# A graph network's attention node stage in five steps a chunk, with the table's bias as a product of a row of ones

## The reference, cut to what matters

```
h = jnp.maximum(_layernorm(x, axis=-1), 0.0)
x = x + _L1_gnn_ref(h, edge_index, ...)      # attention over edges and over each node's own loop, then elu
h = jnp.maximum(_layernorm(x, axis=-1), 0.0)
x = x + _L2_gnn_ref(h, edge_index, W, b)     # its first step is h @ W + b, a table with a row for each node
```

## Time and profile before

| | |
|---|---|
| Median of three runs | 5364.16 us (5360.74 to 5365.61) |
| The profiled execution, its own time | 5366.58 us |
| Its span in the trace | 5364.8 us, clock 0.893 of full speed in the mean |
| The phase of the change, first DMA issue to the next phase's first | 2806.41 to 2995.83 us, 189.4 us or 3.5% of the span |
| 13 chunks in it, from one `attention` to the next | 12.45 us in the mean |

### The profile page before, as it was taken

The page is one execution under the profiler, slowest core; times in us unless marked ns, Lnnn a source line. Parts: engine busy times, 40 slices in busy tenths (PEclk is TensorE's granted clock), DMA queues, the critical chain, the costliest instruction groups (busy, mean ns, idle before and its releaser), DMA issues. The chain is left out here.

```text
span 5364.8 us, 105914 instructions
## 1 busy us (share of the span) xinstructions
PE 4394.3 (82%) x24757; PEld 3537.8 (66%) x24757; DVE 3868.1 (72%) x8472; ACT 1994.7 (37%) x3757; POOL 3403.7 (63%) x3508
## 2 busy tenths in 40 slices
PE   5999999999995888888886555565556899999793
PEld 4888888888775888888874555555555566666431
DVE  5999999999774888788878444444446677777673
ACT  3766766667535555565544200000003000000470
POOL 2677777777516766677730577777764777777473
PEclk8999999999997888889887777777777999999796
DMA  6333333333234555555535333333335111111243
GB/s 199 116 105 102 104 103 103 105 103 105 86 129 126 128 126 126 126 127 127 127 87 157 106 110 109 109 109 109 107 101 166 36 39 39 38 35 29 61 118 105
DMA packets 451779, 555.62 MB, mean 104 GB/s; under 512 B 212912, under 2 KB 321892, under 8 KB 451296
## 3 DMA queue, kind: packets, MB, share of 16 engines
q0 software_dynamic: 154640, 374.88, 25.7%
q1 hardware_dynamic: 289817, 172.07, 11.8%
q10 hardware_dynamic: 6840, 3.36, 0.3%
HBM read 497.40 MB, written 59.40 MB: 104 GB/s over the span
## 5 line engine op out<-in xcount | busy, mean ns | idle before, releaser
L507 POOL DMA_INDIRECT l_rows<-tmp_tab,l_idx x832 | 882.8, 1061 | 376.2 <-issue 252.6
L1217 POOL DMA_INDIRECT l_rows<-tmp_tab,src_sb x832 | 791.6, 951 | 331.8 <-issue 237.4
L1937 POOL DMA_INDIRECT l_rows<-tmp_tab,src_sb x812 | 768.4, 946 | 253.3 <-issue 240.1
L2023 PE MATMUL l_psa<-l_sel,l_rows 128*128 128x128 f32 x3248 | 574.1, 350 | 411.1 <-DVE l_sel L1949 210.9
L2023 PEld LDWEIGHTS l_psa<-l_sel,l_rows 128*128 128x128 f32 x3248 | 532.0, 256 | 453.3 <-issue 238.4
L2175 POOL DMA_INDIRECT l_rows<-tmp_tab,src_sb x695 | 657.1, 945 | 234.3 <-issue 204.1
L805 PE MATMUL l_psw<-l_fw,l_ssp 128*128 128x256 f32 x3328 | 763.4, 382 | 0.0
L1963 DVE TENSOR_TENSOR acc<-acc,l_psa 128x256 f32 x832 | 350.7, 422 | 535.9 <-PE l_psa L2023 454.0
L805 PEld LDWEIGHTS l_psw<-l_fw,l_ssp 128*128 128x128 f32 x3328 | 616.2, 190 | 154.1 <-issue 77.3
L2286 PE MATMUL l_found<-l_tabs,l_hot 128*128 128x384 f32 (+1 forms) x1872 | 650.3, 501 | 0.0
L1537 PE MATMUL l_psa<-l_sel,l_rows 128*128 128x128 f32 x3328 | 605.5, 311 | 52.6 <-DVE acc L1437 51.1
(11 more groups left out here) (362 smaller groups left out, 7717.7 us busy)
## 6 DMA issues: line engine op xcount, KB each, us to landing
l_rows<-tmp_tab,src_sb POOLq DMA_INDIRECT x2339
l_edge<-in_edge_t SPq DMA_DIRECT2D x104, 256.0 KB
l_own<-tmp_tab SPq DMA_DIRECT2D x1280, 1.0 KB
l_own<-tmp_tab ACTq DMA_DIRECT2D x1280, 1.0 KB
l_own<-tmp_tab ACTq DMA_DIRECT2D x1280, 0.2 KB
l_own<-tmp_tab SPq DMA_DIRECT2D x1280, 0.2 KB
tmp_x<-n_X SPq DMA_DIRECT2D x39, 512.0 KB
n_X<-in_x SPq DMA_DIRECT2D x26, 512.0 KB
```

The costliest lines, as they stand in the source:

```text
L507: nc.gpsimd.indirect_dma_start(out=rows[r][:, t, :], out_offset=None, in_=table[:, :], in_offset=bass.IndirectOffsetOnAxis(ap=idx[q][:, j: ...
L1217: nc.gpsimd.indirect_dma_start(out=rows[r][:, j, :], out_offset=None, in_=dram["tab1"][:, :], in_offset=bass.IndirectOffsetOnAxis(ap=sh["s ...
L1937: nc.gpsimd.indirect_dma_start(out=rows[g % ROWS][:, t, :], out_offset=None, in_=table[:, :], in_offset=bass.IndirectOffsetOnAxis(ap=sh["s ...
L2023: last = nc.tensor.matmul(by_tile(g)[0:n, t, k * P:(k + 1) * P], left[:, f:f + n], sel[b][:, t, :], start=True, stop=True)
```

## The change

The same work is spread over five steps and 17 rounds. A round s handles chunk s as `new`, s-1 as `now` (attention, negative, exponential), s-2 as `res` (residual, deviations, shifts), s-3 as `old` (normalize, turn, relu, product) and s-4 as `last` (table). On DVE three chunks are worked on in a round: attention(now), logits(new), residual(res), shares(new), shifts(res). `table` moves to ACT as two copies from PSUM; the bias is put into PSUM by PE, as a product of a row of ones with the bias row ahead of each tile's two products. X and H have three buffers. `psU` has two, for the sums alone, and a single `psX` takes turn and product. SP loads the first attention terms and rows ahead of the weights and the bias, loads the bias to one partition instead of 128, and issues the load of X a round later than that of H. PE and DVE no longer wait for weights and bias at their start.

```diff
-    DEEP = 3
+    RX = 3
-        w, mean_b = ph.sb("w", [P, KH, D]), ph.sb("mean_b", [P, D])
-        X, H, neg, O = (pair_of(ph, n, [P, CT, D]) for n in ("X", "H", "neg", "O"))
+        w, mean_b = ph.sb("w", [P, KH, D]), ph.sb("mean_b", [1, D])
+        X, H = ([ph.sb(f"{n}{r}", [P, CT, D]) for r in range(RX)] for n in ("X", "H"))
+        neg, O = (pair_of(ph, n, [P, CT, D]) for n in ("neg", "O"))
-        ps = ph.ps("psU", DEEP * CT * D)
-        psU = [ps[:, r * CT * D:(r + 1) * CT * D] for r in range(DEEP)]
+        psU = psum_pair(ph, "psU")
+        psX = ph.ps("psX", CT * D)
...
-            for s in range(CHUNKS + 2):
-                step(*(s - j if 0 <= s - j < CHUNKS else None for j in range(3)))
+            for s in range(CHUNKS + 4):
+                step(*(s - j if 0 <= s - j < CHUNKS else None for j in range(5)))
...  SP
+                def logits_in(n):
                     after(sp, share_done, n - 1)
+                    sp.dma_start(att[n % 2][:, :, :], node_rows(dram["att_tab"], n)).then_inc(att_in[n % 2], 16)
+                def rows_in(n):
+                    r = n % RX
+                    after(sp, link_x, n - RX + 1)
+                    sp.dma_start(H[r][:, :, :], node_rows(dram["tab1"][:, 0:D], n)).then_inc(h_in[r], 16)
+                def residual_in(n):
+                    r = n % RX
+                    after(sp, norm_done, n - RX + 1)
+                    after(sp, x_stored[r], 16 * (n // RX))
+                    sp.dma_start(X[r][:, :, :], node_rows(dram["x1"], n)).then_inc(x_in[r], 16)
...
+                def step(new, att_now, res, old, last):
                     if new is not None:
+                        logits_in(new)
+                        rows_in(new)
+                    if new == 0:
+                        ...  w, mean_b (one partition), deg_row
+                    if att_now is not None:
+                        residual_in(att_now)
+                    if res is not None:
+                        residual_out(res)
...  ACT
+                def table(n):
+                    act.wait_ge(mm_done, n + 1)
+                    flat = O[n % 2][:, :, :].rearrange("p t n -> p (t n)")
+                    for lo, hi in BANKS:
+                        last = nc.scalar.activation(flat[:, lo:hi], psX[:, lo:hi], ACT.Copy)
+                    last.then_inc(o_done, 1)
+                def step(new, now, res, old, last):
                     if old is not None:
                         normalize(old)
-                        relu(old)
+                    if last is not None:
+                        table(last)
+                    if now is not None:
+                        negative(now)
                     if new is not None:
                         weights(new)
+                    if old is not None:
+                        relu(old)
+                    if now is not None:
+                        exponential(now)
+                    if res is not None:
+                        deviations(res)
...  DVE: the wait for weights and bias and table(n) are gone
+                def step(new, now, res, old, last):
+                    if now is not None:
+                        attention(now)
                     if new is not None:
                         logits(new)
+                    if res is not None:
+                        residual(res)
+                    if new is not None:
                         shares(new)
+                    if res is not None:
+                        shifts(res)
...  PE: sums does the small transposes first, and no longer waits for table
                 def turn(n):
                     pe.wait_ge(norm_done, n + 1)
-                    pe.wait_ge(h_done, n + 1)
+                    after(pe, o_done, n)
...
                 def product(n):
                     pe.wait_ge(hT_done, n + 1)
+                    for t in range(CT):
+                        out = psX[:, t * D:(t + 1) * D]
+                        nc.tensor.matmul(out, sh["ones"][0:1, :], mean_b[:, :], start=True, stop=False)
+                        for k in range(KH):
+                            last = nc.tensor.matmul(out, hT[n % 2][:, k, t * P:(t + 1) * P], w[:, k, :],
+                                                    start=False, stop=(k == KH - 1))
+                    last.then_inc(mm_done, 1)
```

More of the change, by code:

```diff
@@ L1690, in relu @@
                     for lo, hi in BANKS:
-                        last = nc.scalar.activation(flat[:, lo:hi], psU[n % DEEP][:, lo:hi], ACT.Relu)
+                        last = nc.scalar.activation(flat[:, lo:hi], psX[:, lo:hi], ACT.Relu)
                     last.then_inc(hT_done, 1)
-                def step(new, mid, old):
+                def table(n):
[5 more added lines that the diff above has]
+                def step(new, now, res, old, last):
                     if old is not None:
                         normalize(old)
-                        relu(old)
-                    if mid is not None:
-                        negative(mid)
+                    if last is not None:
+                        table(last)
+                    if now is not None:
+                        negative(now)
                     if new is not None:
                         weights(new)
-                    if mid is not None:
-                        exponential(mid)
-                        deviations(mid)
+                    if old is not None:
[4 more added lines that the diff above has]
+                        deviations(res)
                 unrolled(step)
@@ L1709, in _ @@
             def _(dve):
-                dve.wait_ge(w_in, 32)
                 def logits(n):
@@ L1776, in residual @@
                     last.then_inc(mv_done, 1)
[L1778 to L1785, removed]
                 def shifts(n):
@@ L1840, in product, with step @@
                     pe.wait_ge(hT_done, n + 1)
-                    project(nc, psU[n % DEEP], hT[n % 2], w).then_inc(mm_done, 1)
-                def step(new, mid, old):
+                    for t in range(CT):
+                        out = psX[:, t * D:(t + 1) * D]
+                        nc.tensor.matmul(out, sh["ones"][0:1, :], mean_b[:, :], start=True, stop=False)
+                        for k in range(KH):
+                            last = nc.tensor.matmul(out, hT[n % 2][:, k, t * P:(t + 1) * P], w[:, k, :],
+                                                    start=False, stop=(k == KH - 1))
+                    last.then_inc(mm_done, 1)
+                def step(new, now, res, old, last):
                     if new is not None:
@@ L1847, in step @@
                         turn(old)
+                        if old == 0:
+                            pe.wait_ge(w_in, 16)
+                            pe.wait_ge(b_in, 16)
                         product(old)
```

74 lines of the change are left out of this document (27 added, 47 removed).

## The result

The changed kernel takes 5380.83 us (median of seven runs, 5370.98 to 5392.36), the kernel before 5363.09 (seven runs, 5357.26 to 5366.27): the ratio is 1.0035, with an interval of 1.0025 to 1.0044 (the ratios here are worked out over all runs, so the quotient of the medians can differ in the fourth digit). It is 17.7 us slower, where 5335 was forecast. Its runs also spread over 21 us, against 9 before.

The account below looks back on a forecast made before the run. DVE was taken to set the steady pace, PE's clock adding through ACT. Gains of 2.0 (first attention), 5.0 (first round) and 27.8 (steady stretch), less 5.3 (drain), net 29.5 us: 5335 us, range 5326 to 5351.

Parts of the forecast that it names:

- the price of the ones: On PE, four more bias products a chunk: 0.93 us at most, taking the product from 3.72 to 4.65 us.
- the ring through psX: Product, sums, turn, relu and hand-overs following one another through psX: 8.5 us a round at the high clock, below DVE's 9.92.
- the drain: Last chunks, a chain through the final table: 30.6 us against 25.3 before, a cost of 5.3.
- a PE that is busy keeps its clock: Steady rounds: a late product closes PE's thin stretch, so the clock holds; 0.13 us a round charged for remaining waits.
- DVE's round: Steady rounds: DVE loses the table and the wait for weights, leaving 9.92 us, or 10.05 with a charge for waits.
- The fill: Start of the phase: earlier first loads and small transposes that needn't wait for weights bring first attention 2.0 us earlier.
- First round: First attention to the next: 5.9 us without a residual, against 11.0 before.
- the sum: Whole kernel: gains of 34.8 us less a loss of 5.3, net 29.5 us faster.
- a low product: On PE, a product wholly at low clock takes 8.4 us against 4.65, 3.7 more; half low, it ends 2.1 later.
- rival 3: PE at a low clock replaces DVE as the bound: rounds of 14.2 us, kernel slower at 5391 us; chance 0.07.
- Rival 1: The store of O sets the round at 11.2 us: gain of 17 us, kernel 5347; chance 0.10.
- Against it: Argument against PE as the bound: busy for 13.1 of 14.2 us, PE would see its clock rise.

Follow-up runs that it names:

- experiment 2: The changed kernel with the bias in row 0 of a zero-padded 128-row tile, multiplied by 128 rows of ones: 5333.24 us, ratio 0.9948 to the kernel before.
- experiment 1: The changed kernel without the product of ones, the bias left out of the table altogether: 5329.37 us, ratio 0.9942 to the kernel before.
- experiment 3: The changed kernel with two one-row products of 512 columns ahead of the others, instead of four of 256: 5352.91 us, ratio 0.9983 to the kernel before.
- experiment 9: The changed kernel with two products of 128 rows of ones by 512 columns ahead of the others: 5332.91 us, ratio 0.9947 to the kernel before.
- experiment 8: The changed kernel without ones; DVE adds the bias in the table, at the head of its round: 5363.42 us, ratio 1.0004 to the kernel before.

## Why the prediction was wrong

**What failed is the price of the ones.** "No row has a product with one row of weights. Its bounds are nothing (if it vanishes between the others) and 0.93 for the four; I take the upper end". Three things were missing in it.

- The count. A call is two instructions, which could be read from the x16 of a product's row, for eight calls. With 128 rows the product goes from 3.72 to about 5.4 us, not to 4.65. Price of that alone: experiment 2 less experiment 1, 3.9 us in the medians, where the runs overlap by 2 us.
- The break at each switch of row counts. A tile is 1.68 instead of 1.30 us, the product 6.8 us. At the high clock a round is then 10.32 us, set by the ring through psX, above DVE's 9.96. Over the nine rounds that hold a product that is 0.36 x 9 = 3.2 us, and in the drain 3 x 4 x 0.38 = 4.6 us.
- The clock. At 1.2 GHz the product takes 12.6 us. The two low rounds and those behind them cost 15.6 + 11.4 + 15.4 + 11.5 less 4 x 10.32, which is 12.6 us. In the drain three products cost 3 x 4 x (3.15 - 1.68) = 17.6 us and three turns 2.4. These 32.6 us are gross; experiment 2 lost some 2.9 to low clock as well.

In the two profiled executions the change is behind experiment 2 by 14.6 us in the rounds (131.4 and 116.8) and 23.8 in the drain (55.8 and 32.0), 38.4 in all. The breaks and the clock give 3.2 + 4.6 + 29.7 = 37.5 of that. The medians are 47.6 apart; the 9 us between are in executions without a trace.

The bound was wrong as well as the value: the nearest row for a product bounds it from above only if the neighbours keep their spacing and the clock stays. The range ended below what that mistake could cost.

**Rows and the weight load.** The prediction took from the Trainium skill (TensorE: Matmul & The Clock Gate, LDWEIGHTS) that a load's time goes by columns. The loads themselves agree: 228 ns in the mean with one row, 239 with 128, over both clocks of the change's trace. What the rows cost is the spacing. The Trainium skill (TensorE: Matmul & The Clock Gate, Step-by-step: what each phase is for) ties the pulling ahead of a load to row groups that don't conflict or to a background buffer for weights; with 1, 32 and 64 rows next to 128 the traces show no pulling ahead, 0.33 us of standing loads at each switch, and a tile of 1.68 to 1.69 us.

**The rule on the clock, and the forecast's own.** "a PE that is busy keeps its clock" fell: 38 of 43 us busy, and 0.50 throughout. The Trainium skill (TensorE: Matmul & The Clock Gate, HAM oscillation) explains such falls by idle gaps, long ones above all; as the only cause that doesn't agree with the drain of the change, where PE's longest gap from the last fall on is 1.27 us and the clock stays at 0.50 to the end.

**What held.** DVE's round: 9.92 forecast, 9.96 in experiment 2, with neither the wait nor the table on it. The fill: first attention 4.5 us behind the phase's first issue, where before it was 8.5; 2.0 us less were forecast, 4.0 came, since the first logits were there 1.9 us after their issue (2802.68 to 2804.56). First round 6.1 us for 5.9. The drain 32.0 in experiment 2 for 30.6. And the sum: with ones of 128 rows the kernel is 29.1 us faster, for a forecast of 29.5. That it is so near is in part luck: the fill gave 2.0 us more than forecast, and the longer product and the drain took about as much back. The five steps with the table on ACT did what was worked out, and the one-row product undid it.

Two slips of the prediction's sums had no consequence: half of the 3.7 us that a low product takes longer is 1.9 and not 2.1, and 8.4 + 2.57 + 1.97 is 12.9 us of busy PE in rival 3, not 13.1.

**The rivals.** Rival 1, the store of O: no wait of ACT for it in the change's steady rounds. Rival 3 had the right end, slower, and the right place, PE taking DVE's place with a low clock. Its round of 14.2 us was too short by the count and the break, and its "Against it", that a busy PE raises its clock, is the sentence that kept it at 0.07. Its place was the drain above all, and two of the steady rounds of the profiled execution. That their number differs from one execution to the next would fit the wide spread of the runs, but no trace shows it.

**What stays open.** What keeps the clock down isn't separated into the rows and the breaks. The breaks alone don't bring it down (1.00 through the steady rounds with 32 and 64 rows). Four wide products of one row, with one switch (experiment 3), leave the clock at 0.80 in the steady rounds, 128 rows in the same place (experiment 9) at 0.98; but with no ones at all (experiment 1) it is 0.84, so a fall there doesn't need the one-row products. Why the clock falls when it does, and why the old order suffers more from the ones than the new, wasn't taken apart.

## What to carry to other kernels

A bias put in as a product of one row costs as much of PE as one of 128 rows, breaks the row of pulled-ahead weight loads on both sides, and in turn with full products kept TensorE's clock low once it had fallen. Pad it with zeros to 128 rows, and the same instructions were nearly free here, 3.9 us for 52 calls. Before adding a matrix product of a shape that no row shows, count its instructions in the trace and give its price no upper bound from rows of another shape. Leave room in a round for a product at the low clock: where it fits (experiment 1) it costs nothing, where a ring closes over it (experiment 8) it took most of the gain. When a stage is spread over more steps, work out its drain as a chain: there the buffers saved in the steady rounds are paid back, and two chunks given other buffers at the end took 1.35 us off each of the last two.

## What was unexpected of the hardware

- TensorE at 1.2 GHz while busy 38.12 of 43 us, with one-row and 128-row products in turn.
- Once fallen, the clock stayed low for 3 to 7 us with no ones or ones of 128 rows, and for 14 us or to the end of the phase, 45 us and more, with 1, 32 or 64 rows in turn with 128. With 32 and 64 rows it had stood at 1.00 for some 95 us before.
- A kernel whose clock was 0.84 in the steady rounds (experiment 1) had the same round, 9.96 us, as one at 0.98 (experiment 2).
- 0.33 us of standing weight loads at each switch between 1, 32 or 64 and 128 rows at the high clock, 0.65 at the low one (seen there with 1 row).
- The small first load of 32 KB was in use 1.9 us after its issue when nothing stood ahead of it, against 4.2 us before.
